# Routing rows to the lists of their three experts in the last stage of a two-block decoder

## What is computed

```python
raw_gate = jax.nn.softmax(jnp.einsum('btd,de->bte', x, gate), axis=-1)
_, topk_idx = jax.lax.top_k(raw_gate, 3)
mask = jax.nn.one_hot(topk_idx, 16).sum(axis=2)
gate_topk = mask * raw_gate
gate_topk = gate_topk / jnp.maximum(jnp.sum(jnp.abs(gate_topk), axis=-1, keepdims=True), 1e-12)
hidden = jax.nn.relu(jnp.einsum('btd,edh->bteh', x, W1) + b1)      # 128 -> 256 for each expert
expert_out = jnp.einsum('bteh,ehd->bted', hidden, W2) + b2         # 256 -> 128
return jnp.einsum('bte,bted->btd', gate_topk, expert_out)
```

## Time and profile before

| What | us |
|---|---|
| three runs | 4137.57, 4142.12, 4145.77 |
| median | 4142.12 |
| the profiled execution, its span | 4136.6 |
| PE, DVE, ACT, POOL busy in it | 4001.4, 3384.3, 3291.9, 2648.9 |
| mean granted clock of PE, of full speed | 0.990 |
| DMA: data moved | 46.28 MB |

### The profile page before, as it was taken

The page is one execution under the profiler, slowest core; times in us unless marked ns, Lnnn a source line. Parts: engine busy times, 40 slices in busy tenths (PEclk is TensorE's granted clock), DMA queues, the critical chain, the costliest instruction groups (busy, mean ns, idle before and its releaser), DMA issues.

```text
span 4136.6 us, 148309 instructions
## 1 busy us (share of the span) xinstructions
PE 4001.4 (97%) x61098; PEld 2988.4 (72%) x61098; DVE 3384.3 (82%) x9657; ACT 3291.9 (80%) x9683; POOL 2648.9 (64%) x2257
## 2 busy tenths in 40 slices
PE   7999989999999999999999999999999899999999
PEld 5777756666766777666667667676666588888888
DVE  4667599999889999898899898998999566666665
ACT  3555589989999999999899999999998656666665
POOL 3445488787777777787778777777777433333331
PEclk9999999999999999999999999999999899999999
DMA  3000000000000000000000000000000100000000
GB/s 108 4 4 5 4 3 4 5 3 5 31 5 4 3 31 5 5 4 5 29 5 5 5 31 3 4 5 10 27 10 6 32 4 5 5 5 5 4 4 7
DMA packets 65244, 46.28 MB, mean 11 GB/s; under 512 B 29221, under 2 KB 63033, under 8 KB 63801
## 3 DMA queue, kind: packets, MB, share of 16 engines
q1 hardware_dynamic: 64568, 36.78, 3.1%
HBM read 28.48 MB, written 2.10 MB: 7 GB/s over the span
## 4 chain that ended last, share of the span: by engine, by line
PE 75%; DVE 13%; ACT 8%; issue 2%; POOL 1%; DVEq 0%; SPq 0%; DMA 0%; ACTq 0%; POOLq 0%
PE ps L581 60%; PE ps L585 15%; DVE BIG L1201 6%; ACT BIG L971 5%; DVE sm L1212 3%; ACT BIG L963 2%; DVE BIG L1209 1%; POOL sm L1633 1%; DVE BIG L1206 1%; DVE BIG L1343 0%; POOL BIG L1630 0%; DVE sm L1383 0%; DVE y_sb L1201 0%; DVE sm L1205 0%; DVE BIG L1342 0%
## 5 line engine op out<-in xcount | busy, mean ns | idle before, releaser
L581 PE MATMUL ps<-WB,BIG 128*128 128x128 f32 (+2 forms) x8576 | 1972.1, 364 | 30.8 <-DVE BIG L1209 27.9
L963 ACT ACTIVATE BIG<-ps 128x512 f32<-128x512 f32 (+5 forms) x2784 | 1454.2, 574 | 380.2 <-PE ps L585 222.4
L1630 POOL TENSOR_TENSOR BIG<-BIG,sm 128x512 f32<-128x512 f32 (+1 forms) x864 | 1214.0, 1428 | 601.5 <-DVE sm L1383 302.5
L581 PEld LDWEIGHTS ps<-WB,BIG 128*128 128x128 f32 (+1 forms) x8576 | 1118.1, 191 | 226.3 <-issue 164.4
L585 PEld LDWEIGHTS ps<-t_ident,BIG 128*128 128x128 f32 (+1 forms) x5952 | 709.3, 142 | 428.8 <-issue 294.1
L1630 POOL TENSOR_TENSOR BIG<-BIG 128x512 f32<-128x512 f32 x768 | 960.0, 1276 | 77.6 <-DVE BIG L1201 73.3
L585 PE MATMUL ps<-t_ident,BIG 128*128 128x128 f32 (+1 forms) x5952 | 906.0, 277 | 31.4 <-DVE BIG L1206 9.8
L1212 DVE TENSOR_REDUCE sm<-BIG 128x8 f32<-128x512 f32 (+3 forms) x1472 | 868.0, 617 | 25.5 <-ACT BIG L971 21.7
L581 PEld LDWEIGHTS ps<-BIG 64*64 64x64 f32 (+2 forms) x37888 | 602.4, 128 | 296.7 <-issue 131.4
L581 PE MATMUL ps<-BIG 64*64 64x64 f32 (+4 forms) x37888 | 718.7, 221 | 43.8 <-issue 14.1
L971 ACT ACTIVATE BIG<-ps,sm 128x64 f32<-128x64 f32 (+1 forms) x3104 | 697.5, 392 | 0.6 <-DVE sm L1212 0.6
(11 more groups left out here) (123 smaller groups left out, 2973.8 us busy)
## 6 DMA issues: line engine op xcount, KB each, us to landing
WB<-in_Wqkv SPq DMA_DIRECT2D x6, 1536.0 KB, 7.5
XS<-y_sb SPq DMA_DIRECT2D x96, 63.0 KB
y_sb<-in_ctx SPq DMA_DIRECT2D x16, 256.0 KB, 3.5
WB<-in_Wo SPq DMA_DIRECT2D x6, 512.0 KB, 9.0
x_sb<-in_x SPq DMA_DIRECT2D x8, 256.0 KB, 5.0
WB<-in_F_W SPq DMA_DIRECT2D x1, 2048.0 KB, 9.8
WB<-in_F_W SPq DMA_DIRECT2D x8, 256.0 KB, 4.8
out<-x_sb SPq DMA_DIRECT2D x8, 256.0 KB, 2.3
```

The lines of the kernel that those rows point to most:

```text
L581: return te.matmul(o, l, r, start=start, stop=stop, skip_group_check=not check)
L963: return se.activation(o, i, ACT.Copy)
L1630: return pe_.tensor_tensor(o, a, b, op)
```

## The change

In the last stage the experts leave the tile loop. For each tile DVE makes a mask of 3 x 16 (oh), its sum over the three (mb), and a running count of rows for each expert (cu); PE makes each row's rank in its expert's list from a triangular matrix and the counts so far (rk); DVE turns rank and expert into a row number (rk, sl, s3, ix). ACT copies xn3 twice (xr), so that a tile has three copies of its rows, each with two more numbers: where its result is to go (id, POOL) and its weight (gg). POOL scatters the three copies by three indirect DMAs of 128 rows of 520 bytes to the lists in DRAM, `xg` (sc). A list has room for 4096 rows for each expert; all are filled with harmless rows beforehand by 71 transfers that SP starts during layers two to six (`clear`).

After the tiles a unit FT works out a table with the first row of each of the 111 pages: 3 x 4096 rows are 96 pages, and each of sixteen lists may end in one that is partly filled. For each page SP waits for a buffer, loads the page's row number from the table into a register, and starts two loads with it: the page (128 x 520 bytes) and its expert's weights (128 x 2056 bytes). Then a unit FB transposes the page (PE, DVE), runs the two products and the Relu (PE, ACT), scales by the weight (DVE), and POOL scatters 128 rows of 512 bytes to `zg` by an indirect DMA. When all have landed, SP reads the results back in eight transfers, and units FC add the three results of each row to x (POOL, DVE) before the output.

There are eight load buffers and four for results. The order of DE is a new one on all engines, with lags up to 16 where they were up to 7, and `SLOT` and `BEGIN` for it differ. The buffers of the last part are now three where they were two. The experts' weights stay in DRAM in a new layout, one block for each expert.

```diff
+NE = 16
+CAP = 4096
+TOK = NT * 128
+PAGES = (3 * TOK + NE * 127) // 128
+XROWS = NE * CAP + PAGES * 128
+NXB, NYB = 8, 4
+ZROWS = 3 * TOK + (NE + PAGES) * 128
...
-    "pe": "T2 oF6 oG6 hD5 hJ6 G3 s2 oH6 hK6 J1 oJ6 oI6 hL6 p02 hN6 hM6 ct3 om3 hA5 oK6 oL6 p12 av3 u2 hO6 X10 "
-          "hP6 oM6 t2 gT5 oN6 oA5 w2 oB5 b25 oO6 oP6 oC5 hE5 xc2 hF5 X34 oD5 hH5 hG5 g2 g34 oE5 hC4 hB4 hI5 cs2",
...
-    "dve": "qn3 xD7 ge4 h25 ab4 m36 su6 ls4 rc6 rg6 ti6 v15 id6 xE7 cf6 cs4 gj4 e06 xF7 xG7 v25 dm4 mx4 c03 "
...
-    "pool": "v36 d25 m04 m14 bo4 h56 h66 pw24 pw36 pw11 gb4",
+    "pe": "cta w8 J6 cs9 ava gTc p17 G9 p07 xc8 b2c X3b g3b T6 om9 u7 g8 rkb t7 s6 X15",
+    "act": "e18 e08 sq7 ln7 lx7 gTd p18 p08 xc9 X3c exa h2b x3c T7 xrc g19 ema t8 vc9 X16 g29 cta",
+    "dve": "ti7 v16 su7 id7 md5 v26 gs7 cf7 gm7 oh7 r3 mb7 n3 xn11 gr7 gg7 cu7 st10 ge4 rk7 ab4 ag10 sl7 h46 c12 ls4 s37 "
+           "c02 cs4 gj4 a1 w3 v1 og7 ix7 x6 ss1 st23 a05 ag23 ep10 st36 n01 a15 ag36 ep36 a25 ep23 a35 dm4 xn23 mx4 a45 "
+           "xn36 hh5 b27 mm4 s15 qn1 s25 h25 m36 C4",
+    "pool": "idg bob h5f h6f m1b gbd m0b pw2c pw3f pw19 d2d scg v3e",
 }
...
+FB_ORDER = {"pe": "T0 h1 o3", "act": "h1", "dve": "T0 o3", "pool": "z3"}
+FT_ORDER = {"pe": "c0 o0", "act": "", "dve": "c0 f0 g0 d0 u00 u10 u20 u30 h0 m0 r0 o0 q0 t0", "pool": ""}
+FC_ORDER = {"pe": "", "act": "", "dve": "x0 y0", "pool": "s0"}
...
-SLOT = {"ab": 13.426, "c": 11.263, "de": 25.04}
...
-    "de": {"pe": 3196.38, "act": 3166.88, "dve": 3167.24, "pool": 3145.67},
+    "de": {"pe": 3160.99, "act": 3153.23, "dve": 3221.04, "pool": 3110.00},
+    "ft": {"pe": 5000.0, "act": 5000.0, "dve": 5000.0, "pool": 5000.0},
+    "fb": {"pe": 5100.0, "act": 5100.0, "dve": 5100.0, "pool": 5100.0},
+    "fc": {"pe": 6000.0, "act": 6000.0, "dve": 6000.0, "pool": 6000.0},
...
-    "de": "0G=2 0hE=1 0w=2 0xc=4 1J=7 1t=1 1xc=5 2X1=3 2p0=2 2t=2 2xc=8 3p0=9 3xc=1",
+    "de": "0G=2 0w=2 0xc=4 1t=1 1xc=5 2X1=3 2p0=2 2t=2 2xc=8 3p0=9 3xc=1",
...
-            def expert_weights_1():
-                eng.dma_start(WB[:, 0:4096].rearrange("p (e h) -> p e h", e=16),
-                              din["F_W1"].rearrange("e d h -> d e h")).then_inc(sems["wm1"], 16)
-
-            def expert_weights_2():
-                for i in range(8):
-                    eng.dma_start(WB[:, 4096 + 512 * i:4608 + 512 * i].rearrange("p (e k d) -> p e k d", e=2, k=2),
-                                  din["F_W2"][2 * i:2 * i + 2].rearrange("e (k p) d -> p e k d", p=128)).then_inc(sems["wm2"], 16)
+            def clear(n):
+
+                if n < 64:
+                    e, p = n // 4, 1024 * (n % 4) + CAP * (n // 4)
+                    eng.dma_start(xg[p:p + 1024, :].rearrange("(b p) c -> p b c", p=128),
+                                  din["F_empty"][e].unsqueeze(1).broadcast_to([128, 8, 130])).then_inc(sems["empty"], 16)
+                elif n < 71:
+                    k = 16 * (n - 64)
+                    m = min(16, PAGES - k)
+                    eng.dma_start(xg[NE * CAP + 128 * k:NE * CAP + 128 * (k + m), :],
...
+            def blocks():
+
+                for s in qkv_free(depth - 1) + [uC2[(depth - 1, 7)].on("pe", "o"), FT[0].on("dve", "t")]:
+                    w.wait_ge(*s)
+                for p in range(3):
+                    w.wait_ge(f"xr{p}", 48 * len(range(p, NT, 3)))
+                for j in range(PAGES):
+                    if j >= NXB:
+                        w.wait_ge(*FB[j - NXB].on("pe", "o"))
+                        w.wait_ge(f"ys{(j - NXB) % NYB}", 16 * ((j - NXB) // NYB + 1))
+                    at = eng.value_load(table[0:1, j:j + 1], min_val=0, max_val=XROWS - 128)
+                    eng.dma_start(XB[j % NXB], xg[bass.ds(at, 128), :]).then_inc(sems[f"bw{j % NXB}"], 16)
+                    eng.dma_start(FW[j % NXB], din["F_W"][bass.ds((at >> 12) * 128, 128), :]).then_inc(sems[f"bw{j % NXB}"], 16)
+
+            def results():
+                for p in range(NYB):
+                    w.wait_ge(f"ys{p}", 16 * len(range(p, PAGES, NYB)))
+                for g in range(8):
+                    eng.dma_start(BIG[:, 1536 * g:1536 * g + 1536].rearrange("p (t c) -> p t c", t=4),
+                                  zg[1536 * g:1536 * g + 1536, :].rearrange("(t p i) d -> p t (i d)", p=128, i=3)).then_inc(sems[f"x{g}"], 16)
...
                         shift(l, g)
+                        if l:
+                            clear(2 * (8 * l + g - 8))
+                            clear(2 * (8 * l + g - 8) + 1)
...
                         if g >= 2 and l == depth - 1 and "E" in stages:
                             context(g - 2)
                         if g == 2 and l == depth - 1 and "F" in stages:
-                            expert_weights_1()
-                if "F" in stages:
-                    for s in qkv_free(depth - 1):
-                        w.wait_ge(*s)
-                    expert_weights_2()
+                            routing()
...
+            blocks()
+            results()
...
-                elif ph[0] == "h":
-                    c = 256 * EXPERTS.index(ph[1])
-                    w.wait_ge("wm1", 16)
-                    w.wait_ge(*u.on("act", "X3"))
-                    mm(K[:, 0:128], WB[:, c:c + 128], b.xT3)
-                    o = mm(K[:, 128:256], WB[:, c + 128:c + 256], b.xT3)
...
-                    mm(K[:, 0:128], b.hid[e_ % 4][:, 0:128], WB[:, c:c + 128], stop=False)
-                    o = mm(K[:, 0:128], b.hid[e_ % 4][:, 128:256], WB[:, c + 128:c + 256], start=False)
+                    o = mm(K[:, 0:128], b.GT, T["F_b2"][:, :])
+                elif ph == "rk":
+                    w.wait_ge("lists", 2)
+                    w.wait_ge(*u.on("dve", "mb"))
+                    o = mm(K[:, 0:16], strict, b.M, stop=not t)
+                    if t:
+                        w.wait_ge(*DE[t - 1].on("dve", "cu"))
+                        o = mm(K[:, 0:16], allone, seen[t % 4], start=False)
...
+            def pe_fb(u, ph):
+                j = u.at["j"]
+                for v, e, m in u.after[ph]:
+                    w.wait_ge(*v.on(e, m))
+                K, W = bank[u.bank[ph]], FW[j % NXB]
+                if ph == "T":
+                    w.wait_ge(f"bw{j % NXB}", 32 * (j // NXB + 1))
+                    o = tr(K[:, 0:128], XB[j % NXB][:, 0:128])
+                elif ph == "h":
+                    w.wait_ge(f"bw{j % NXB}", 32 * (j // NXB + 1))
+                    w.wait_ge(*u.on("dve", "T"))
+                    for n in range(2):
+                        o = mm(K[:, 128 * n:128 * n + 128], W[:, 128 * n:128 * n + 128], XT[j % 4])
+                elif ph == "o":
+                    w.wait_ge(*u.on("act", "h"))
+                    for n in range(2):
+                        o = mm(K[:, 0:128], HID[j % 4][:, 128 * n:128 * n + 128], W[:, 256 + 128 * n:384 + 128 * n], start=not n, stop=bool(n))
+                o.then_inc(u.name("pe", ph, sems), 1)
...
-                elif ph[0] in "hk":
...
-                    o = act(b.hid[e_ % 4][:, 128 * half:128 * half + 128], bank[u.bank["h" + ph[1]]][:, 128 * half:128 * half + 128], ACT.Relu,
-                            bias=T["F_b1"][:, 2 * e_ + half:2 * e_ + half + 1])
...
+                elif ph == "xr":
+                    w.wait_ge(*u.on("dve", "xn3"))
+                    o = copy(b.XR[:, 1:3, 0:128], bc_mid(b.xn3, 2))
...
+                for n in range(2):
+                    o = act(HID[j % 4][:, 128 * n:128 * n + 128], K[:, 128 * n:128 * n + 128], ACT.Relu, bias=W[:, 512 + n:513 + n])
...
                     if t >= places:
                         w.wait_ge(*DE[t - places].on("pe", last))
+                        if ph == "xn3":
+                            w.wait_ge(f"xr{t % 3}", 48 * (t // 3))
+                            w.wait_ge(*DE[t - 3].on("pe", "rk"))
+                            w.wait_ge(*DE[t - 3].on("dve", "og"))
...
-                elif ph == "rc":
-                    w.wait_ge(*u.on("dve", "su"))
-                    o = ve.reciprocal(sm[:, 1, 2:3], sm[:, 1, 1:2])
-                elif ph == "rg":
-                    w.wait_ge(*u.on("dve", "rc"))
-                    o = ts(b.L, b.L, sm[:, 1, 2:3], None, ALU.mult)
                 elif ph == "ti":
...
-                elif ph == "e0":
+                elif ph == "oh":
                     w.wait_ge(*u.on("dve", "cf"))
-                    if t >= 2:
-                        w.wait_ge(*DE[t - 2].on("dve", "xP"))
-                    o = ts(b.M, T["iota"][:, :], sm[:, 3, 0:1], None, ALU.is_equal)
-                elif ph in ("f1", "f2"):
-                    w.wait_ge(*u.on("dve", "e0" if ph == "f1" else "f1"))
-                    o = stt(b.M, T["iota"][:, :], sm[:, 3, int(ph[1]):int(ph[1]) + 1], b.M, ALU.is_equal, ALU.add)
-                elif ph == "gk":
-                    w.wait_ge(*u.on("dve", "f2"))
-                    o = tt(b.M2, b.M, b.L, ALU.mult)
```

(42 more changed lines are left out.)

278 lines of the change are left out of this document (211 added, 67 removed), and 8 rows, old and new, of tables (DE_EMPTIED, DE_ORDER).

## The result

The changed kernel takes 4219.64 us (median of 4 runs, 4212.69 to 4224.81), the kernel before 4140.31 beside it. The ratio is 1.0191, 95% interval 1.0173 to 1.0208: slower by 1.9%, where 4076 was forecast. The profiled execution has a span of 4223.0 us.

A forecast was written before the change was run, and what follows sets the result against it. TensorE, 97% busy, bounds the kernel before. Last b2 3753, page table 4, first page 7, pages 278, results 4 + 21 + 5 + 1 make 4073 us profiled, 4078 as median, stated as 4076; range 3950 to 4215.

The forecast's parts named there:

- I take 13.0 us for a tile: Tile loop: DVE and POOL tie as the busiest engines, so a tile takes 13.0 us, bounds 12.5 and 16.2.
- rival D: Tile loop: the clock stays near 0.65, PE needs 15.4 us a tile, 74 us more, 4150; chance 0.07.
- PE's work, 10.2 us: Tile loop: 10.0 us of PE left a tile without the experts, plus some 0.2 for the rank's matmuls.
- PE near 80% at clock 1.0: Tile loop: a listed sign that the forecast is right, PE's busy share at full granted clock.
- DVE, 12.5: Tile loop: DVE's work a tile, 17.7 - 5.5 - 1.2 + 1.5 = 12.5 us.
- POOL, 12.6, with 1.3 for a scatter: Tile loop: POOL's work a tile, 8.7 us plus three indirect scatters of 1.3 us each.
- Rival B: Tile loop: POOL holds each scatter for 2.5 us, a tile takes 16.2 us, 99 us more, 4175; chance 0.14.
- The fill: Start of the last stage: 80 us plus 10 for the low clock, first tile's b2 at 3350.
- The pages, 2.5 each: Page stage: SP's issues 0.95, register load 1.2, waits and arithmetic 0.35 us; 111 pages take 278 us.
- The rings do not bind: Page stage: eight load buffers against a round of about 10 us allow 1.25 us a page.
- Results, page table: After the tiles, page table 4 us; after the pages, results 4 + 21 + 5 + 1 us.
- dear pages: Page stage, a rival: SP's load, waits and arithmetic take 2.8 us, 3.75 a page, 139 more, 4215; chance 0.16.

The follow-up runs named there:

- e1: The changed kernel with 16 idle 128x128 matmuls per tile put in TensorE's waits of the last stage; 4182.92 us.
- e4: The changed kernel with expert weights loaded for the first eight pages only, later pages reusing what their buffer holds; 4140.5 us.
- e3: The changed kernel with sixteen load buffers for pages instead of eight; 4162.01 us.
- i3: e3 and h1 combined, plus 25 idle matmuls a tile, odd pages loaded from ACT's queue and seven result buffers; 4069.09 us, ratio 0.9813 to the kernel before.
- g1: The changed kernel with G ahead of gT and om ahead of T in TensorE's order of the tile loop; 4203.1 us.
- h1: g1 with DVE's og and ix moved ahead of c0 and cs; 4206.2 us.

## Why the prediction was wrong

The mechanism failed in one step, "DVE (12.5) and POOL (12.6) tie; PE has 2.3 us of slack at full clock ... I take 13.0 us for a tile". The step takes the busiest engine's work plus 0.5 for the period. The earlier trace rows stand for a stretch in which another order kept DVE full; nothing in the working asked whether the new lists let PE and DVE overlap. The chain above did not: PE and DVE took turns, and the granted clock of 0.66, which the sum left to rival D, stretched PE's turn from 6.3 to 10.75 us.

- **PE's work, 10.2 us:** right at full clock (10.7 by e1). At the granted 0.66 it was 80.16 x 0.2047 = 16.4 us. "PE near 80% at clock 1.0", a sign of being right, came with the wrong clock.
- **DVE, 12.5:** too low. It was 13.9 (14.5 at full clock), in the main from waits beside POOL that a sum of durations out of other stretches can't hold.
- **POOL, 12.6, with 1.3 for a scatter:** right, but by luck. The 1.27 us was borrowed from a 512-wide multiply; a scatter takes 0.96 to 1.38 us and 0.30 of gap, and no run ties the two together. POOL holds 12.3 us a tile. Rival B is out. The Trainium skill's 2.0 us plus bytes ("DMA: Bandwidth & Descriptors", Anatomy of one DMA), an estimate of 2.15 us for these 67 KB, is met by the time to landing at its shortest (2.2 to 4.3 us for the 66 KB scatters in e4's chain, 4000 to 4040 us). POOL is free for most of it, as the prediction read it: its next scatter starts after 1.27 us.
- **The clock.** Rival D named it and gave PE 15.4 us a tile, but then took PE as the bound and 4150 as the end, and had it as "self-limiting, since a slow PE becomes a busy one". PE needed 16.4 us and waited 4.1 more: at the low clock it still waits, for DVE's C ahead of om and for DVE's og ahead of gT. D had a chance of 0.07; it is half of what happened, the alternation with DVE being the other half.
- **The sizes.** The first 25 periods average 19.73 us, which is 25 x 6.73 = 168 us over the forecast; the loop's end gives about 6 of them back, and 163 are left. Of the 6.73, e1's tiles at full clock leave 16.1 - 13.0 = 3.1 us, 78 us in 25 periods, to the chain and DVE's waits, and 19.73 - 16.1 = 3.6 us, 91 us, to the clock. This is a split by one kernel that has idle matmuls on its chain, so the first part is at most 78. By the spread of the kernels with the same loop the clock's part is 2.1 to 4.1 us a tile.
- **The fill:** first b2 at 3365.47 against 3350, 15 us late, with a granted clock of 0.65 and 0.69 in 3260 to 3300. How much of it the clock cost was not separated.
- **The pages, 2.5 each:** too dear. SP's load, waits and arithmetic were put at 1.55 us and took 0.76, so 1.65 a page. The Trainium skill's floor of 600 ns for a register load (the same page, Latency and other measured facts) fits this, and the 1.9 us a page worked out from it is nearer to SP's pace than my 2.5. The pages as a whole took 2.19 us each. "The rings do not bind" was wrong: with the lag of three and two rings in a row, waits for buffers cost e3's 48 us, and the four result buffers more. With 1.65 us a page the forecast's own sum would be 289 - 94 = 195 us; measured are 261.6. That the two errors partly cancel is luck.
- **Results, page table:** right, 30.3 against 31 us, 5 against 4. **Clears:** free; the layers kept their times (SP's last shift is issued at 3091.46, before at 3097.81, and the first big projection of the last stage runs at 3261.44, before at 3259.97).

Sum: 15.5 + 162.7 for fill and tiles, -27.4 for table and pages, -0.7 for results: 150, and 4073 + 150 = 4223, the span. That this lies only 5 us above the range's top of 4215 says nothing for the range: its top stood for dear pages, and the pages were cheaper than forecast.

The change itself pays once its pace is not given away: i3, the same algorithm, beats the kernel before by 1.9% (interval 1.7 to 2.0) and the changed one by 3.6% (4069.09 / 4219.64).

What stays open: how long a tile would be if PE's and DVE's lists overlapped. No order tried here did more than trim DVE's waits; with the clock held, PE's own filling (16.2 of 17.1 us) is now the bound, and fewer idle matmuls let the clock go. Whether g1's and h1's orders give anything at the low clock is open too, as each ran once. And why the same loop averages 18.2 us a tile in one kernel and 20.15 in another was not found.

## What to carry to other kernels

When a change empties the engine that set the pace, the new period is not the next engine's work: follow one tile of the new order through the in-order lists and add the stretches in which one engine waits for the other. Price the emptied TensorE at both clock levels, with its waits kept. And where several short rings and queues follow one another, expect each repair to show nothing until the last limit near the same pace is gone: four kernels at 207 to 216 us stood before the one at 161.

## What the runs showed of the hardware that was not expected

- Work that does nothing made the kernel faster: 25 idle matmuls of 0.23 us in each tile moved the granted clock in the loop from 0.64 to 0.72 up to 0.95 to 1.00, and a steady tile from an average of 18.2 to 20.15 us (seven kernels) to one of 17.2 to 17.9 (six kernels). With 16 to 20 the clock went back and forth between its levels.
- A GpSimd multiply of 1.25 us holds up a DVE operation on two SBUF operands to its own end (0.21 becomes 1.31 us), and leaves one with a PSUM operand alone. In h1, moving the victim only picked another one.
- An indirect scatter of 128 rows of 512 bytes holds GpSimd for 0.97 us, and the next follows 0.30 us later: 1.27 us, as i3 keeps it for over 30 scatters in a row.
- A transfer whose address comes from a register costs SP 0.33 us for the issue, no more than one with a fixed address (0.43 us in the earlier trace rows). Fetching the address, with the waits and arithmetic around it, costs more than twice that, 0.76 us a page.
